# Cross-attention scores in pieces of 64 queries, with only the keys that their band reaches

## What is computed

```python
    x = x + attn(layernorm(x))                       # 16 heads of 8
    x = x + xattn(layernorm(x), ctx, ctx, wq, wk, wv, wo)
    x = x + ffn(layernorm(x))                        # 8 experts and a shared one

def xattn(q, k, v, wq, wk, wv, wo):                  # H, DH, W = 16, 64, 32
    qh, kh = rope(q @ wq.T), rope(k @ wk.T)          # by head
    scores = jnp.einsum('bhqd,bhkd->bhqk', qh, kh) * DH ** (-0.5)
    i, j = jnp.arange(l)[:, None], jnp.arange(l)[None, :]
    scores = jnp.where((j <= i) & (j >= i - W), scores, -1e+30)
    probs = jax.nn.softmax(scores, axis=-1)
    return (probs @ vh) @ wo.T
```

## Time and profile before

| | us |
|---|---|
| median of 3 runs | 792.15 (792.11 to 793.57) |
| profiled execution, its own time | 793.52 |
| span in the trace | 790.7 |
| TensorE matmul busy | 759.4 (96%) |
| TensorE weight loads busy | 631.8 (80%) |
| VectorE busy | 536.6 (68%) |
| ScalarE busy | 539.2 (68%) |
| GpSimd busy | 535.4 (68%) |

### The profile page before, as it was taken

One profiled execution on the slowest core, in us unless ns is written; L12 is line 12 of the kernel. 1 busy time (PEld: TensorE's weight loads), 2 busy tenths in 40 slices (PEclk: granted clock), 3 DMA queues, 4 the chain that ended last, 5 costly groups with the idle time before them and its releaser, 6 DMA issues.

```text
span 790.7 us, 28613 instructions
## 1 busy us (share of the span) xinstructions
PE 759.4 (96%) x10349; PEld 631.8 (80%) x10349; DVE 536.6 (68%) x1350; ACT 539.2 (68%) x1900; POOL 535.4 (68%) x864
## 2 busy tenths in 40 slices
PE   7999999999999999999999999999899999999894
PEld 4778878888888888888888888888679778777563
DVE  3466767777777777777777777777866686665553
ACT  1367767777777777777777777777667667666352
POOL 3366777777777777777777777777565666576434
PEclk8999999999999999999999999999999999999998
DMA  6013212222222222222222222223043132133130
GB/s 232 12 56 124 80 61 82 88 91 93 92 93 73 73 73 73 72 73 73 73 73 73 73 73 72 73 73 128 9 129 125 48 101 72 40 104 123 55 101 12
DMA packets 56791, 64.06 MB, mean 81 GB/s; under 512 B 4014, under 2 KB 52916, under 8 KB 56656
## 3 DMA queue, kind: packets, MB, share of 16 engines
q1 hardware_dynamic: 52928, 54.06, 20.9%
q0 software_dynamic: 3008, 6.57, 2.4%
q10 hardware_dynamic: 720, 1.63, 0.5%
HBM read 17.80 MB, written 45.35 MB: 80 GB/s over the span
## 4 chain that ended last, share of the span: by engine, by line
PE 91%; DVE 3%; issue 2%; DMA 1%; ACT 1%; POOL 1%; SPq 0%; POOLq 0%; DVEq 0%; ACTq 0%
PE P L327 8%; PE P L272 8%; PE P L307 7%; PE P L292 7%; PE P L316 7%; PE P L338 7%; PE P L282 7%; PE P L397 5%; PE P L224 4%; PE P L207 4%; PE P L356 4%; PE P L239 4%; PE P L247 2%; PE P L364 2%; PE P L410 1%
## 5 line engine op out<-in xcount | busy, mean ns | idle before, releaser
L799 ACT ACTIVATE PX<-P,mx 128x128 f32<-128x128 f32 x512 | 182.1, 394 | 61.0 <-DVE mx L569 61.0
L966 POOL TENSOR_TENSOR PX<-PX,mx 128x512 f32<-128x512 f32 x128 | 133.0, 1041 | 62.0 <-DVE mx L574 62.0
L569 DVE TENSOR_REDUCE mx<-P 128x4 f32<-128x512 f32 x128 | 82.0, 679 | 119.3 <-PE P L307 119.3
L799 ACT ACTIVATION_READ_ACCUMULATOR PX<-P,mx 128x1 f32 x512 | 119.9, 234 | 0.0
L763 ACT ACTIVATE PS<-P 128x512 f32<-128x512 f32 x128 | 66.1, 602 | 32.0 <-PE P L228 32.0
L999 POOL DMA_INDIRECT out<-yst,xrow x46 | 46.0, 1000 | 54.6 <-DVE yst L673 42.5
L508 DVE TENSOR_REDUCE nmf<-P 128x4 f32<-128x512 f32 x128 | 79.5, 683 | 5.1 <-PE P L207 2.2
L961 POOL TENSOR_TENSOR rq<-rq,tq 128x1024 f32<-128x1024 f32 x32 | 75.7, 2365 | 8.8 <-DVE tq L533 7.8
L808 ACT ACTIVATE PT<-P 128x512 f32<-128x512 f32 x128 | 77.7, 607 | 3.5 <-PE P L316 0.8
L956 POOL TENSOR_TENSOR rk<-rk,tk 128x1024 f32<-128x1024 f32 x32 | 75.5, 2359 | 0.0
L272 PE MATMUL P<-wvT,cxT 128*128 128x512 f32 x128 | 70.4, 633 | 3.0 <-DVE tk L533 3.0
(11 more groups left out here) (144 smaller groups left out, 1757.4 us busy)
## 6 DMA issues: line engine op xcount, KB each, us to landing
z_xs<-c SPq DMA_DIRECT2D x34, 1088.0 KB, 5.3
xrow<-z_xs SPq DMA_DIRECT2D x46, 136.0 KB, 2.1
ew<-in_ew SPq DMA_DIRECT2D x9, 384.0 KB, 6.4
x<-in_x SPq DMA_DIRECT2D x32, 64.0 KB, 1.8
cxT<-in_ctxT SPq DMA_DIRECT2D x31, 64.0 KB, 1.7
out<-yst,xrow POOLq DMA_INDIRECT x46, 2.3
wk<-in_wk SPq DMA_DIRECT2D x1, 512.0 KB, 4.4
wvT<-in_wvT SPq DMA_DIRECT2D x1, 512.0 KB, 7.0
```

The lines of the kernel that those rows point to most:

```text
L569: dve.tensor_reduce(mx[b % 3][:, 0, r, :], v3(bank(f"ds{r}")), AX.X, ALU.max, negate=True).then_inc(S["v_dm"][r], 1)
L799: t = act.activation(PX[(4 * b + r) % 6][:, c, :], p[:, c * 128:c * 128 + 128], ACT.Exp, bias=m[:, 0, r, c:c + 1], scale=1.0, accum_out=m[ ...
L966: pool.tensor_tensor(X[:, :, :], X[:, :, :], mx[b % 3][:, 2, r, :].rearrange("p (h a) -> p h a", a=1).to_broadcast([128, 4, 128]), ALU.mul ...
```

## The change

In d_s each product of 128 queries by 128 keys becomes two: the queries 0 to 63 with the keys 0 to 63, written to the partitions 0 to 63 and columns 0 to 63 of the head's part of the bank, and the queries 64 to 127 with the keys 32 to 127, written to the partitions 64 to 127 and columns 32 to 127. The mask is written over all 128 by 128 as before, so a place without a product holds the mask alone. The array is thereby used in pieces of 32 rows by 64 columns for these products, where it was 32 rows by 128 columns. The order of the steps, the waits and the banks are the same.

```diff
+
                 for c in range(4):
                     for e in range(2):
-                        for r in range(4):
-                            t = pe.matmul(p[r][:, c * 128:c * 128 + 128], rq[b % 2][32 * r:32 * r + 32, e, c, :],
-                                          rk[b % 2][32 * r:32 * r + 32, e, c, :], start=False, stop=(c == 3 and e == 1),
-                                          skip_group_check=True)
+                        for u, first in ((0, 0), (1, 32)):
+                            for r in range(4):
+                                t = pe.matmul(p[r][64 * u:64 * u + 64, 128 * c + first:128 * c + 64 * u + 64],
+                                              rq[b % 2][32 * r:32 * r + 32, e, c, 64 * u:64 * u + 64],
+                                              rk[b % 2][32 * r:32 * r + 32, e, c, first:64 * u + 64], start=False,
+                                              stop=(c == 3 and e == 1), skip_group_check=True)
                 t.then_inc(S["t_ds"], 1)
```

## The result

The changed kernel takes 812.59 us (median; 810.90 to 814.34) where the kernel before takes 792.13 us beside it: a ratio of 1.0255, 95% interval 1.0227 to 1.0284. It is slower, as forecast, but by 20.5 us and not by 7.4, and it lies above the range of 781 to 808. The profiled execution took 813.67 us with a span of 810.9, 20.2 us more than before.

The account below looks back on a forecast made before the run. TensorE was taken to bound the kernel. Shorter scores gave -10.6 us and instruction-fetch stops +18, together +7.4 on the median of 792.15: 799.5 us, range 781 to 808, chance of slower 0.70.

Parts of the forecast that it names:

- What bounds: In the steady part TensorE is busy nearly always, so time it saves or loses passes to the end one to one.
- The gap of shape: Between L299 and the scores, a new array partition costs a 0.09 us gap plus 0.05 for the first weight load.
- Shorter scores: Scores' products with halves side by side: 1.34 us against 1.78; net saving 0.33 us a batch, 10.6 us in 32.
- the longer half sets the time: In the scores, halves running side by side take only the 96-key half's 16 passes of 0.084 us, 1.34 us.
- Stops behind the scores in the steady part: In L239 or the output projection, waits for instruction blocks of 256: 14.3 us over sixteen batches, up to 1.36 each.
- The beginning and the end: Outside the sixteen stopping batches: no stops forecast in the sixth to eleventh batches, 4 us given to the last five.
- the price of a boundary inside the scores: For the last five batches' block boundaries: one stop at 1.6 us, two near 1.2, the rest nothing.
- late packets: Instruction packets delayed as in the two old gaps; some of these, with packets 0.4 us later, make stops 26 us.
- The stops don't come: Rival: packets go out earlier or more instructions lie ready, leaving only the saving, 781.6 us; chance 0.21.
- The halves in turn: Rival: in the scores, column halves run one after the other within a row group, about 815 us; chance 0.08.
- Supply too slow: Rival: TensorE can't take the scores' instructions that fast; 800 us (0.03) or 850 us (0.01), chance 0.04 together.

Follow-up runs that it names:

- the first experiment: The changed kernel with 31 warm-up products fewer ahead of the first batch (36 become 5), moving the block boundaries: 798.68 us, ratio 1.0068 to the kernel before.

## Why the prediction was right about the sign and wrong about the size

**What bounds: right.** TensorE's losses went to the end nearly one to one. No other engine became the bound.

**The gap of shape: right.** It was priced at 0.09 us and a first load of 0.05, 0.14 together. From the last start of L299 to the first of L309 are 0.144 us where it was 0.047, so 0.10 were added; from the first L299 matmul to L309 it is 0.33 where it was 0.23.

**Shorter scores: the mechanism right, the size wrong.** 1.34 us for 16 rounds was the price of the longer half alone, and alone it does about that: L239 starts 1.81 us after the first L299 matmul, where 1.83 was forecast. The step "the longer half sets the time" failed: with both halves first to last start is 1.546 us and not 1.308. A rival named the supply of instructions, at 7 ns each from L299's row; the lowest that any run shows is 5 ns, and the changed kernel is at 6.0. I gave it 0.03. It can't be the whole of it, for between 1.27 and 1.55 us the columns still count; how much of it is supply the runs leave open. The saving is 0.16 us a batch, 5.1 us and not 10.6: 5.5 us of the miss.

**Stops behind the scores in the steady part: right.** The prediction let them begin with about the thirteenth batch and gave 14.3 us in sixteen batches, up to 1.36 each. Between the 11th and the 26th start of the scores 313.64 us pass, where 15 periods without a stop take 302.21: 11.4 us, and with the 27th batch's 1.2 it is 12.6. They start in the twelfth batch and reach 1.4 (the 22nd). Of the net change 8.5 us fall here (+1.4 to +9.9 in the table above); the steps of the prediction give about 8, -0.33 x 15 and some 13 of stops. Part of that agreement is luck: the saving was too large and the stops as well. The inference from two torn groups and a count (blocks of 256, one of them ahead) held: each stop of the changed kernel in or just behind the scores (L309, L239, L378 to L382, L341) falls on the first instruction of a block, and when a block is entered the trace has had the packets up to its own and none for a later one. (Two of the experiments' kernels have one stop of 0.35 us in the 32nd batch's scores that stands elsewhere in its block.) In those of the 12th to 25th batches a block was used 2.85 to 3.7 us after the first instruction of the one before, 2.2 to 2.7 of it after the packet's start. The prediction took 3.6 us after the scores' start.

The packet of the stop at 543.55, by the slice of 541.1:541.3 in which it stands (2.4 us ahead, as in the earlier trace rows):

```profile
DMA  0000000000090000000000000000000000000000
```

The Trainium skill ("Advanced Engine Details and Errata", ISA Cache) has cache lines of 16 KB or 256 instructions and only two of them, but in the same place 128 KB for TensorE, which would hold eight. What the traces show, one block ahead, fits two; the 2.85 to 3.7 us from one entry to the next block's use only the runs give.

**The beginning and the end: wrong.** For the first ten batches the steps give -3.3 us (saving only), the table has +1.4; for the last seven batches and what follows about +3 (4 us of stops in the last five, 1.4 in the 27th, less 2.3 saved), and the table has +10.3. Here three steps failed. One is the price of a boundary inside the scores: "nothing" or 1.2 to 1.6 us was given, and single records show 2.1 in the 28th, 0.9 in the 31st and 2.3 in the 32nd batch, and 1.5 behind the 30th's scores. In the 28th and 32nd the block before is entered 0.15 and 0.2 us ahead of the scores, so nearly all of its 256 instructions are theirs and nothing slower stands among them. The second is that late packets were thought of as rare and as old as the kernel. While the DMA engines are full from before a block's entry the packet went out 3.6 us after it in the second batch and some 4.3 us in the 26th, where the same boundary had its packet 1.1 us after the entry in the 25th and 27th. Here is DMA in 557.2:563.2 (0.15 us a slice); the block ahead of the stop at 561.8 to 563.8 is entered at 557.1, and the packet goes out at 561.4:

```profile
DMA  9999999999999999999999999992567412001000
```

The kernel before has that traffic too and stopped at the same place for 1.63 us, and for 1.05 us in the mask of the fourth batch; the changed kernel stops 2.4 us in the second instead, inside the scores, and in the twenty-sixth 2.0 and 0.6. Dense instructions have no slack to give to a late packet. The third is a term that the prediction put at nothing: what a long stop does to the clock. Four times the granted clock fell to 0.50 for 3.4 us behind a stop, for some 5.5 us together, 1.5 of them in the first ten batches and 4 in the last seven. The stops of 1.3 and 1.9 us of the kernel before, measured by the delay of the first matmul behind them, were followed by no such fall.

**The rivals.** "The stops don't come" (0.21) falls with the timelines of the changed kernel; the first experiment ties them to the blocks. "The halves in turn" falls with the 1.83 us of 128 keys each, where 3.3 were expected of turns. "Supply too slow" may be right in part, as said.

## What to carry to other kernels

Before a product is cut into smaller ones that run side by side, count the instructions: each f32 piece is two loads and two matmuls. A block of 256 that is used up in less than 2.9 to 3.7 us, measured here in the stretches around the scores, stops the engine for the rest of that time, however short each instruction is made, and where it stops depends on the offset of everything ahead of it. A stop of some 2 us cost up to 1.5 us more here, by the clock. If such a stretch is wanted, move the boundaries (the count of a filler is enough, worth 14 us here) and keep large transfers away from it; without that, less work gave more time.

## What the runs showed that I had not expected

- Eight pieces of 32 x 64 do run at once; loads and matmuls together went at 5 ns each at best (1.27 us for 256).
- Less work for the same instructions gave no less time: second halves of 96, 64 and 32 keys end within 2.1 us of one another.
- The page's busy TensorE (94%) hides it: 20 us of loss show as 2% less in the share, and as 3% of "issue" in the chain.
- A packet of 16 KB is not released by the entry of the block before alone. Around the scores of the changed kernel's 12th to 25th batches it starts at the entry or up to 1.4 us after it; where the engines are full from before the entry, 3.0 to 4.4 us after it in the stops of the 2nd and 26th batches of this kernel and of the first experiment. But where TensorE takes some 13 us for a block it starts 2.6 to 4.5 us after the entry with the engines idle. Here is DMA in 292.3:297.3 of the changed kernel (0.125 us a slice), with the block entered at its start and the next one needed at 305.9; what starts the packet then stays open:

```profile
DMA  0000000000000000000000000000000400000000
```

- In no stop was a block used earlier than 2.2 us after its packet's start.
